# Two-layer network, second layer: matmuls of a down part and of the next up part issued in turn, each into another PSUM bank

## What is computed

```python
def _L1_ffn_ref(x, up, down, perm):        # H, Dh, M = 16, 128, 512
    unperm = jnp.argsort(perm)
    t = x.reshape(b * l, Dm)[:, perm].reshape(b * l, h, d)
    t = jnp.einsum('bhd,hdm->bhm', t, up)
    t = jax.nn.gelu(t, approximate=False)
    t = jnp.einsum('bhm,hmd->bhd', t, down)
    out = t.reshape(b * l, h * d)[:, unperm].reshape(b, l, Dm)
x = x + _L0_ffn_ref(_L0_cond_ref(x, ...), ...)
x = x + _L1_ffn_ref(_L1_cond_ref(x, cond_128, ..., fside_S_0), L1_ffn_up, L1_ffn_down, L1_ffn_perm)
```

## Time and profile before

| | us |
|---|---|
| median of 3 runs | 2611.23 |
| lowest, highest | 2610.18, 2614.82 |
| profiled execution, span of the page | 2612.7 |
| TensorE busy | 2564.3 (98%) |
| weight loads | 2106.0 (81%) |
| VectorE busy | 1836.2 (70%) |
| ScalarE busy | 1002.5 (38%) |
| GpSimd busy | 952.1 (36%) |
| down matmuls, 1536 rows (L1406) | 212.4 + 201.0 + 200.0 |
| up matmuls, 1416 rows (L1396, operands t_hi, t_lo) | 187.1 + 186.1 + 184.4 |

### The profile page before, as it was taken

One profiled execution on the slowest core, in us unless ns is written; L12 is line 12 of the kernel. 1 busy time (PEld: TensorE's weight loads), 2 busy tenths in 40 slices (PEclk: granted clock), 3 DMA queues, 4 the chain that ended last, 5 costly groups with the idle time before them and its releaser, 6 DMA issues.

```text
span 2612.7 us, 39106 instructions
## 1 busy us (share of the span) xinstructions
PE 2564.3 (98%) x12090; PEld 2106.0 (81%) x12090; DVE 1836.2 (70%) x2667; ACT 1002.5 (38%) x1632; POOL 952.1 (36%) x826
## 2 busy tenths in 40 slices
PE   8999999999999999999999999999999999999997
PEld 6788888888888888887888778888888788888775
DVE  6665555965556754576444768888888888888876
ACT  3221212321122322232222555555555555555573
POOL 2366645466654455232233212222222222222221
PEclk9999999999999999999999999999999999999998
DMA  9955544665545677576455654576767676777687
GB/s 316 317 194 203 197 162 154 235 208 194 192 161 180 222 225 222 160 249 208 150 170 182 204 172 131 158 221 210 224 207 222 206 223 210 223 224 218 210 275 244
DMA packets 417282, 541.03 MB, mean 207 GB/s; under 512 B 36248, under 2 KB 270064, under 8 KB 417072
## 3 DMA queue, kind: packets, MB, share of 16 engines
q1 hardware_dynamic: 314816, 307.40, 39.6%
q10 hardware_dynamic: 78144, 154.27, 15.7%
q0 software_dynamic: 24112, 76.80, 9.3%
HBM read 309.72 MB, written 228.61 MB: 206 GB/s over the span
## 4 chain that ended last, share of the span: by engine, by line
PE 91%; DVE 3%; DMA 3%; issue 2%; SPq 1%; ACT 1%; ACTq 0%; DVEq 0%; POOLq 0%; POOL 0%
PE ps_c L459 45%; PE ps_up L1396 13%; PE ps_y L1406 13%; PE ps_c L1421 9%; PE ps_v L437 4%; PE ps_c L425 2%; PE ps_zt L1434 2%; PE ps_f L1442 2%; DVE w_lo L1002 1%; PE ps_up L1421 1%; DVE ring_lo L949 0%; SPq L85 0%; DMA x_n<-in_up 0%; DMA u_s<-z_d,idx 0%; DMA aggw_d<-agg 0%
## 5 line engine op out<-in xcount | busy, mean ns | idle before, releaser
L459 PE MATMUL ps_c<-w_hi,ring_hi 128*128 128x512 f32 x1792 | 712.8, 398 | 2.1 <-DVE r_early L998 1.2
L459 PE MATMUL ps_c<-w_hi,ring_lo 128*128 128x512 f32 x1792 | 706.9, 394 | 0.0
L459 PE MATMUL ps_c<-w_lo,ring_hi 128*128 128x512 f32 x1792 | 706.7, 394 | 0.0
L609 ACT ACTIVATE ring_hi<-raw_n 128x512 fp32r<-128x512 f32 x382 | 239.6, 631 | 874.3 <-DVE raw_n L940 237.6
L1378 POOL DMA_INDIRECT y_d<-y_s,idx x128 | 145.8, 1139 | 728.5 <-ACT y_s L1546 676.8
L1503 ACT ACTIVATE kern<-ps_up 128x512 f32<-128x512 f32 x512 | 306.7, 599 | 262.1 <-PE ps_up L1396 249.2
L459 PEld LDWEIGHTS ps_c<-w_hi,ring_hi 128*128 128x128 f32 x1792 | 337.8, 188 | 80.5 <-DVE ring_lo L949 3.3
L459 PEld LDWEIGHTS ps_c<-w_hi,ring_lo 128*128 128x128 f32 x1792 | 337.5, 188 | 78.9
L459 PEld LDWEIGHTS ps_c<-w_lo,ring_hi 128*128 128x128 f32 x1792 | 337.8, 189 | 75.6
L1620 DVE TENSOR_TENSOR g_lo<-kern,g_hi 128x512 fp32r<-128x512 f32 x512 | 354.7, 693 | 38.7 <-ACT g_hi L1507 22.2
L998 DVE TENSOR_TENSOR r_early<-ps_c,r_early 128x512 f32<-128x512 f32 x256 | 176.7, 691 | 283.2 <-PE ps_c L459 283.2
(11 more groups left out here) (211 smaller groups left out, 3841.2 us busy)
## 6 DMA issues: line engine op xcount, KB each, us to landing
u_d<-raw_n ACTq DMA_DIRECT2D x64, 512.0 KB, 3.3
x_d<-r_early ACTq DMA_DIRECT2D x128, 256.0 KB, 3.5
raw_n<-u_d SPq DMA_DIRECT2D x64, 512.0 KB, 3.6
x_d<-x_s ACTq DMA_DIRECT2D x126, 256.0 KB, 2.7
u_s<-x_d SPq DMA_DIRECT2D x496, 64.0 KB, 2.1
z_d<-x_s SPq DMA_DIRECT2D x120, 256.0 KB, 3.8
rear<-y_d SPq DMA_DIRECT2D x112, 256.0 KB, 3.1
rear<-x_d SPq DMA_DIRECT2D x112, 256.0 KB
```

What stands on the lines that cost most here:

```text
L459: mm = nc.tensor.matmul(bank, a[:, dc, :], w[k][:, dc, :], start=(first and dc == 0 and n == 0), stop=(dc == 3 and n == 2), skip_group_che ...
L609: nc.scalar.activation(ring_hi[g % RING][:].rearrange("p a n -> p (a n)"), factor(q, k, p), ACT.Copy).then_inc(hi_ready, 1)
```

## The change

`up_part` and `down_part` become one function, `feed_forward(k, h, mc)`. It takes the waits of the down part (of step s) and of the up part (of step s + 1) first, and then issues the six matmuls in turn: one into `ps_y`, one into bank mc of `ps_up`, three times over. The operands, the order inside each part and the signals with each part's last matmul stay. `skip_group_check` concerns the build alone.

```diff
--- before.py
+++ after.py
@@ -1386,27 +1386,34 @@
 
         @block.tensor
         def _(pe):
-            def up_part(k, h, mc):
-                s = H * k + h
-                if mc == 0:
-                    pe.wait_ge(tlo_ready, s + 1)
-                wait(pe, gelu_done, MC * (s - 1) + mc + 1)
-                hi, lo = t_pair(k, h)
-                for n, (w, t) in enumerate(((w_hi, hi), (w_hi, lo), (w_lo, hi))):
-                    mm = nc.tensor.matmul(ps_up[:, mc, :], chunk(w, 2 * h)[:, mc * P:(mc + 1) * P], t,
-                                          start=(n == 0), stop=(n == 2))
-                mm.then_inc(up_done, 1)
-
-            def down_part(k, h, mc):
-                s = H * k + h
-                pe.wait_ge(glo_ready, MC * s + mc + 1)
-                if mc == 0:
-                    wait(pe, y_ready, s)
-                for w, g in ((w_hi, g_hi), (w_hi, g_lo), (w_lo, g_hi)):
-                    mm = nc.tensor.matmul(ps_y[:, 0, :], chunk(w, 2 * h + 1)[:, mc * P:(mc + 1) * P], g[:, mc, :],
-                                          start=(mc == 0 and w is w_hi and g is g_hi),
-                                          stop=(mc == MC - 1 and w is w_lo))
-                mm.then_inc(down_done, 1)
+            def feed_forward(k, h, mc):
+
+                down, up = exists(k, h, 0), exists(k, h, 1)
+                if down:
+                    s = H * k + h
+                    pe.wait_ge(glo_ready, MC * s + mc + 1)
+                    if mc == 0:
+                        wait(pe, y_ready, s)
+                if up:
+                    k2, h2 = after(k, h)
+                    s2 = H * k2 + h2
+                    if mc == 0:
+                        pe.wait_ge(tlo_ready, s2 + 1)
+                    wait(pe, gelu_done, MC * (s2 - 1) + mc + 1)
+                    hi, lo = t_pair(k2, h2)
+                for n in range(3):
+                    if down:
+                        w, g = ((w_hi, g_hi), (w_hi, g_lo), (w_lo, g_hi))[n]
+                        mm = nc.tensor.matmul(ps_y[:, 0, :], chunk(w, 2 * h + 1)[:, mc * P:(mc + 1) * P], g[:, mc, :],
+                                              start=(mc == 0 and n == 0), stop=(mc == MC - 1 and n == 2), skip_group_check=True)
+                        if n == 2:
+                            mm.then_inc(down_done, 1)
+                    if up:
+                        w, t = ((w_hi, hi), (w_hi, lo), (w_lo, hi))[n]
+                        mm = nc.tensor.matmul(ps_up[:, mc, :], chunk(w, 2 * h2)[:, mc * P:(mc + 1) * P], t,
+                                              start=(n == 0), stop=(n == 2), skip_group_check=True)
+                        if n == 2:
+                            mm.then_inc(up_done, 1)
 
             def conv(k, h):
                 u, j, b, g = conv_unit(k, h)
@@ -1453,10 +1460,7 @@
                     pe.wait_ge(wsplit_lo, CHUNKS)
                     pe.wait_ge(z_ready, LEAD)
                 for mc in range(MC):
-                    if exists(k, h, 0):
-                        down_part(k, h, mc)
-                    if exists(k, h, 1):
-                        up_part(*after(k, h), mc)
+                    feed_forward(k, h, mc)
 
             drive(pe, step)
             for v in range(H):
```

## The result

| | us |
|---|---|
| kernel before, median of 4 runs | 2611.18 (2610.18 to 2614.82) |
| kernel after, median of 4 runs | 2651.45 (2649.77 to 2653.75) |
| ratio | 1.0152, 95% interval 1.0139 to 1.0164 |
| forecast | 2637 (2618 to 2655), slower |

What follows compares the result with a forecast made beforehand. TensorE was taken to bound the kernel (91% of the chain). Middle 6.1, first stage 7.8, last stage 11.9 and end 0.5, alternation 0, sum to 26.3 us: 2637 us against the 2611.2 median, range 2618 to 2655.

Steps and rivals of the forecast that it cites:

- The sign and the places: Second layer's steps: slower by 1.0%, D0 idle until t_lo releases it, mostly in first and last stages; slower 0.87.
- The later y copy: End of each step: D3's last matmul and the y copy 0.46 us later, GELU 3 and t_lo +0.25.
- The release: D0's wait for t_lo: weight load starts 0.05 us behind t_lo's end.
- Middle steps: s = 17 to 107: mostly +0.03 us a step, 8.50 to 8.55 each; 6.1 us together with late ones.
- The late steps: Two middle steps with a late t: 0.7 us at one, some 0.8 at the other.
- Last stage: s = 108 to 127: D0 closes the t_lo loop, 6.88 us a turn instead of 6.19; 11.9 us in all.
- alternation costs: Rival, all matmuls: each bank switch adds up to 10 ns, 9 to 29 us, 2646 to 2666; chance 0.10.
- Alternation hides something: Rival, between matmuls: 15.5 ns each come back, 45 us, giving 2592 us; chance 0.07.
- GELU 3 doesn't slide: Rival, ScalarE and VectorE: wait moves without GELU 3's delay, 17.5 us, 2629 or 2621; chance 0.20.
- the clock falls: Rival, last stage: new idle drops TensorE to the lower clock level, 70 us, 2707; chance 0.03.
- nothing moves: Rival, D0's wait: something hides it, time stays within 0.2%, 5 us; chance 0.04.

Runs made afterwards that it cites:

- e4: Changed kernel with matmuls back in the old order (three down, three up), all waits still ahead of D's first matmul: 2637.9 us, 1.0110.
- e5: Changed kernel with GELU 3 issued ahead of the y copy in steps up to s = 108: 2657.4 us, 1.0172.
- e1: Changed kernel with t_lo's wait called first in unrolled steps, so it stands last, on the weight load: 2642.8 us, 1.0117.
- e7: Changed kernel with t_lo's wait on the load everywhere, GELU 3 before the y copy up to s = 108, last-stage t split behind mc = 0: 2639.5 us, 1.0102.
- e3: Changed kernel, matmuls still alternating, but waits for t_lo and GELU taken just ahead of U's own first matmul: 2627.2 us, 1.0068.
- e11: e5, but with the y copy ahead of GELU 3 again for the last head of each block: 2643.5 us, 1.0118.
- e8: e5 with GpSimd gathering t three steps ahead, not two, from s = 31 on: 2649.2 us, 1.0136.
- e9: Kernel before with last-stage t split behind mc = 0 and the gather three steps ahead: 2611.5 us, 0.9995.
- e10: e7 with the gather of t three steps ahead: 2640.4 us, 1.0103.
- e2: Changed kernel with t_lo's wait called first in all steps, loop included: 2649.5 us, 1.0152.
- e6: Kernel before with last-stage t rounded and split behind mc = 0, not mc = 2: 2611.6 us, 0.9989.

## Why the prediction was right, and where it was too small

- **The sign and the places: right.** TensorE waits at D0 for t_lo, in the first and last stages above all, with the clock at its upper level.
- **The later y copy: right in size.** In the middle step above it starts 0.20 behind the start of U3's last matmul, and before it started 0.26 ahead of that (2004.55 against 2004.81): the 0.46 of the forecast. GELU 3 follows it by 0.50. Steps with and without it (after and e4, after and e5) are 0.25 apart in the first stage, as forecast.
- **The release: mis-sized, the step that failed.** "The price of a release ... so 0.05 behind" is right for the loop, for e1 and for the earlier trace rows, where U0's t_lo wait stood on the load itself. In the some 60 unrolled steps of after it is 0.23. I read the rows of a wait that was one of two and applied them to one of four, though the order of the instructions showed where it stood. A first-stage step is 8.05 + 0.21 (D0 waits, e7) + 0.25 (late copy) + 0.17 (late release) = 8.68, as measured. The forecast of 8.5 lacks the last term, and e1 has exactly that step, 8.52.
- **Middle steps.** The forecast, 8.50 to 8.55, holds in the loop (8.512) and in e1 (8.50). The unrolled ones are 0.18 over it, for the same reason. That is 26 x 0.18 = 4.7 of the 4.9 us too few (11.0 against 6.1, s = 108 apart). The late steps came out near their price: s = 50, 57, 64, 96 and 98 lose some 4.5 us, against 2.3 for s = 64 and 65 of before, so 2.2 more, where the forecast had 1.5.
- **Last stage: too small as well, 11.9 against 14.8.** The 12.5 in the table lies near the forecast only because the table counts the step up to s = 108 as middle. I said 6.88 a step, it is 7.09, and e1, with the release as I priced it, has 6.91. The step up to s = 108 alone lost 2.3 us, where the sum had 0.9 for the first of the stage and one other. It has no convolution before D0 to cover the wait for t_lo, and its t isn't rounded ahead, so it takes 8.68, as a first-stage step does. Against that, three steps that had taken 7.3 to 8.0 before (s = 109, 111, 113) took 7.1 after: a stall that was there anyway took in the new one, 1.3 us back.
- **The price of e1 in all**, 8.7 of the 40 us, and the 5 us between executions come near the distance between 26 and 40. What else was off (s = 108, the late steps, the 1.3 us back, 1.0 less ahead of s = 0 and 0.7 less at the end) nearly cancels.
- **The range.** 2651 lies above the 2626 to 2648 that the forecast's own mechanism had been given. It is inside 2618 to 2655 only because that range took in the lower half of *alternation costs*, which did not happen. That part is luck.

**The rivals.** *Alternation hides something* and *alternation costs* both fall: starts in the loop of after are as far apart as before. From the first row to the second are 14 starts,

```profile
2181.08 0.39 PE L1413 MATMUL ps_up<-t_lo,w_hi 128*128 128x512 f32 x1
...
2184.28 0.39 PE L1413 MATMUL ps_up<-t_hi,w_lo 128*128 128x512 f32 x1
```

3.20 / 14 = 0.2286 each, against the 0.2295 that I had used, and e3 shows a whole step the same. 2651 lies in the range that I gave to the costly rival, but for another reason. *GELU 3 doesn't slide* falls with e4 and e5, *the clock falls* with the windows, *nothing moves* with the result. The warm gap of 215.8 ns that the Trainium skill gives for 512 columns (TensorE: Matmul & The Clock Gate, "Back-to-back issue gap"), there for a matmul by itself, was not reached by alternating banks: the starts stayed at 228.6 ns. The warning of cycling through PSUM banks in the Trainium skill (TensorE: Matmul & The Clock Gate, "A second HAM failure mode: psum-queue depth-cycling") did not come true here, the granted clock being 1.00 in all three windows.

**The late steps, as far as the traces show.** In every kernel that has t_lo's wait on D0, s = 64 alone loses 2.5 to 3.0 us, and s = 65 another 1.6 to 1.8 in e1, e7 and e11; in before and e3, s = 64 and 65 together lose 2.3 to 2.4. s = 64 is where the loop jumps back for its second turn. On VectorE the jump stands at 2098.3 us of after, its next instruction at 2101.3, and t_lo behind that:

```profile
L1137 DVEq COMPARE_BRANCH  x2: 55/59/63, 2098.3 to 2373.9; - x2
```
```profile
2101.48 0.69 DVE L1584 TENSOR_TENSOR t_lo<-u_s,t_hi 128x512 fp32r<-128x512 f32 x1 [2.52 <-issue]
```

All thirteen kernels have this pause at the jump, 2.8 to 3.4 us long; the exit from the loop (2373.9) has 0.1. Where s = 57 is late (in e3 s = 58), it is for a pause on GpSimd: the scatter of s = 55 starts 3.49 us behind its copy of y and not 0.81, and the gather of t queued behind it lands late.

```profile
2031.89 0.99 POOL L1378 DMA_INDIRECT y_d<-y_s,idx  x1 [8.80 <-issue]
```
```profile
2038.36 0.63 ACT L1501 ACTIVATE t_hi<-u_s 128x512 fp32r<-128x512 f32 x1 [0.96 <-DMA u_s<-z_d,idx]
```

The same 3.49 stand in every kernel but e8, e9 and e10, which have the edit of the gather; in before, e2 and e6 no step comes late for it.

**What stays open:** what the engines do in these pauses; why other single steps come late in e7, e8, e10 and e11; and where the time of e5 lies in the executions that were not profiled. The variants that shorten every step lose most of it to late ones.

## What to carry to other kernels

Taking the waits of two chains together at the head of both makes the first matmul wait for the later chain: count what stood between the two waits, for that is the cover that goes. Where several waits stand on one instruction, let the one that comes last stand on the instruction itself, and look in the assembled order where it is; here that was worth 0.17 us each time, 9 us in all. And a matmul that signals may not be moved back without a look at who waits for the signal: 0.46 us at the end of D3 came back as 0.25 in every step of the first stage.

## What was not expected of the hardware

- With the wait met last standing first of four on one TensorE instruction, 0.23 us pass from the end of t_lo to the load; with it last, 0.06. In the first case the trace has two semaphore instructions in between, 0.11 apart, and the load 0.07 behind the second.
- Writing two PSUM banks in turn, every matmul, left the distance of starts at 0.229 us and the middle step at 8.473 us.
- ScalarE's rows follow each other by 0.50 us though each lasts 0.60, y copy to GELU, as in the earlier trace rows (0.47).
- The loop's jump back costs VectorE 2.8 to 3.4 us from the branch to its next instruction, in every kernel here; with t_lo's wait on D0 the step there, s = 64, loses 2.5 to 3.0 us.
